# A projected column's residual: ScalarE reads the column twice, GpSimd subtracts, VectorE keeps the first stream's columns

## The reference

```
q = heads(q_in @ wq + bq)
k = heads(k_in @ wk + bk)
scores = einsum('bhqd,bhkd->bhqk', q, k) / sqrt(16)
```

## Time and profile before

| | us |
|---|---|
| median of three runs | 1411.68 (1407.81 to 1411.82) |
| span of the profiled execution, first to last instruction | 1379.5 |
| PE busy / VectorE / ScalarE / GpSimd, of the span | 1255.7 / 888.8 / 663.2 / 523.9 |

### The profile page before, as it was taken

The page is one execution under the profiler, slowest core; times in us unless marked ns, Lnnn a source line. Parts: engine busy times, 40 slices in busy tenths (PEclk is TensorE's granted clock), DMA queues, the critical chain, the costliest instruction groups (busy, mean ns, idle before and its releaser), DMA issues. The chain is left out here.

```text
span 1379.5 us, 18247 instructions
## 1 busy us (share of the span) xinstructions
PE 1255.7 (91%) x5694; PEld 569.1 (41%) x5694; DVE 888.8 (64%) x2045; ACT 663.2 (48%) x1243; POOL 523.9 (38%) x731
## 2 busy tenths in 40 slices
PE   6898989989999999999999999998899888999996
PEld 3232433323343224453453444443242334666663
DVE  5889789788877986458557567568768423233332
ACT  2355455566555655556546556446656551012221
POOL 4444251163312411326217227225423122456665
PEclk9799999999999999999999999999999999999998
DMA  8472513324330333033123123124622004934341
GB/s 262 131 245 81 159 49 96 109 65 147 110 106 24 108 93 108 22 87 108 47 63 108 47 62 108 47 62 123 139 85 48 17 16 118 337 99 55 55 54 16
DMA packets 113216, 131.53 MB, mean 95 GB/s; under 512 B 17017, under 2 KB 93305, under 8 KB 112867
## 3 DMA queue, kind: packets, MB, share of 16 engines
q1 hardware_dynamic: 102867, 119.91, 30.0%
q0 software_dynamic: 10256, 10.45, 4.6%
HBM read 83.25 MB, written 48.40 MB: 95 GB/s over the span
## 5 line engine op out<-in xcount | busy, mean ns | idle before, releaser
L1288 DVE TENSOR_REDUCE Mx<-bank 128x1 f32<-128x512 f32 x512 | 339.0, 685 | 206.6 <-PE bank L1022 204.5
L904 ACT ACTIVATE prob<-bank 128x512 f32<-128x512 f32 x576 | 332.4, 594 | 257.2 <-PE bank L1048 255.6
L1048 PE MATMUL bank<-QS,KS 99*128 99x512 bf16 x768 | 296.1, 387 | 40.1 <-ACT prob L904 19.5
L1022 PE MATMUL bank<-KS,QS 96*128 96x512 bf16 x768 | 296.9, 388 | 14.2 <-DVE Mx L1285 8.0
L1061 PE MATMUL bank<-prob,V 128*17 128x512 f32 x1536 | 206.6, 610 | 0.7 <-ACT prob L904 0.7
L904 ACT ACTIVATE prob<-prob 128x512 f32<-128x512 f32 x192 | 120.9, 629 | 159.4 <-DVE prob L1299 158.5
L1048 PEld LDWEIGHTS bank<-QS,KS 99*128 99x128 bf16 x768 | 74.8, 98 | 234.2 <-ACT prob L904 130.3
L1022 PEld LDWEIGHTS bank<-KS,QS 96*128 96x128 bf16 x768 | 76.0, 99 | 123.0 <-issue 47.2
L1285 DVE CUSTOM_DVE_ANT_0 bank<-bank,ff_h 128x512 f32<-128x512 f32 x128 | 87.9, 696 | 20.6 <-PE bank L1022 20.0
L741 POOL TENSOR_SCALAR parts<-rest 128x512 bf16<-128x512 f32 x47 | 29.1, 620 | 183.4 <-DVE rest L1248 182.8
L727 POOL TENSOR_SCALAR shift<-mv 128x4 f32<-128x4 f32 x28 | 5.5, 197 | 233.5 <-DVE mv L1209 233.5
(11 more groups left out here) (180 smaller groups left out, 1833.2 us busy)
## 6 DMA issues: line engine op xcount, KB each, us to landing
stack_scr<-parts SPq DMA_DIRECT2D x48, 384.0 KB, 2.6
QS<-stack_scr SPq DMA_DIRECT2D x47, 384.0 KB, 4.1
KS<-stack_scr SPq DMA_DIRECT2D x47, 384.0 KB, 5.0
stack_scr<-parts SPq DMA_DIRECT2D x48, 256.0 KB, 2.9
w_gu<-in_gate_up SPq DMA_DIRECT2D x16, 512.0 KB, 9.6
stack_scr<-parts SPq DMA_DIRECT2D x48, 128.0 KB, 2.9
cT<-in_ctxT SPq DMA_DIRECT2D x8, 512.0 KB, 5.8
w_dn<-in_down SPq DMA_DIRECT2D x16, 256.0 KB, 10.0
```

Of the source, the lines that this page charges most:

```text
L904: act.activation(prob[:, u % NP_, j, :], src, ACT.Exp, scale=CAST).then_inc(exp_done, 1)
L1022: pe.matmul(m, QS[0:STACK, h, qt * P:(qt + 1) * P], KS[0:STACK, h, :], start=True, stop=True).then_inc(s_full, 1)
L1048: pe.matmul(bankT[e % NT][:, :], KS[0:ROWS, h, kt * P:(kt + 1) * P], QS[0:ROWS, h, :], start=not on_pe, stop=True).then_inc(t_full, 1)
L1288: dve.tensor_reduce(dst, b, AX.X, ALU.max).then_inc(s_read, 1)
```

## The change

For all streams but the first (44 of the 48 columns):

- ScalarE reads the column twice, in two instructions one behind the other: once for part 0 (bf16), once as a whole with the bias into `rest` (fp32). The second frees the M bank, and counts in ScalarE's `m_read`; `head_ready` isn't counted any more.
- GpSimd waits for that count instead of VectorE's, subtracts part 0 from `rest` in place (a third instruction ahead of its two), and goes on as before.
- VectorE does nothing for these columns. In `jobs_read` the bank now goes back at `head`, not at `cut`.

Stream 0's four columns stay as they were.

```diff
--- before.py
+++ after.py
@@ -322,7 +322,10 @@
     read_by_act = {"hT": "turn", "aT": "attT", "relu": "ff1", "swish": "gate"}
     if kind in read_by_act:
         return "act", [(read_by_act[kind], *at)]
-    made = {"val": "v", "cut": "col", "i8turned": "i8T", "top": "logits", "route": "rank"}
+    if kind in ("head", "cut"):
+        return ("dve", [("col", *at)] if kind == "cut" else []) if at[0] == 0 else \
+            ("act", [("col", *at)] if kind == "head" else [])
+    made = {"val": "v", "i8turned": "i8T", "top": "logits", "route": "rank"}
     if kind == "add":
         return "dve", [("out", *at)]
     if kind == "i8add":
@@ -738,6 +741,8 @@
                         return
                     s, r = parts[:, j % 2, :, :], rest[:, j % 2, :]
                     read_done(pool, ("col", n, what, m))
+                    if n:
+                        link(pool.tensor_tensor(r, r, s[:, 0, :], ALU.subtract))
                     link(pool.tensor_scalar(s[:, 1, :], r, 1.0, 0.0, ALU.mult, ALU.add))
                     pool.tensor_tensor(s[:, 2, :], r, s[:, 1, :], ALU.subtract).then_inc(part_ready, 1)
 
@@ -868,8 +873,12 @@
                     if j >= 2:
                         act.wait_ge(part_out[j % 2], 48 * (j // 2))
                     act.wait_ge(m_full, i + 1)
-                    act.activation(parts[:, j % 2, 0, :], bankM[BANK[("col", n, what, m)]][:, :], ACT.Identity,
-                                   bias=b_qk[:, n // B, "qk".index(what), m:m + 1]).then_inc(head_ready, 1)
+                    b, bias = bankM[BANK[("col", n, what, m)]][:, :], b_qk[:, n // B, "qk".index(what), m:m + 1]
+                    if n:
+                        act.activation(parts[:, j % 2, 0, :], b, ACT.Identity, bias=bias)
+                        act.activation(rest[:, j % 2, :], b, ACT.Identity, bias=bias).then_inc(m_read["act"], 1)
+                    else:
+                        act.activation(parts[:, j % 2, 0, :], b, ACT.Identity, bias=bias).then_inc(head_ready, 1)
 
                 def minus(i):
 
@@ -1362,7 +1371,7 @@
                         largest(*at)
                     elif kind == "merge":
                         merge(*at)
-                    elif kind == "cut":
+                    elif kind == "cut" and at[0] == 0:
                         cut(*at)
                     elif kind == "val":
                         take_values(*at)
```

## The result

| | before | after |
|---|---|---|
| median of all runs on one chip, us | 1411.59 (1407.81 to 1413.62, 6 runs) | 1420.92 (1416.99 to 1423.35, 6 runs) |
| ratio | 1 | 1.0071, 95% interval 1.0052 to 1.009 |

The change makes the kernel 0.7% slower, 9.3 us. I had forecast no difference, 1411, with a range that ended at 1420.

The account below looks back on a forecast made before the run. The prediction took TensorE, nearly full and working in order, to bound the kernel through its stalls. Its terms summed to +0.1 us on a 1379.5 us span; with 32.2 us outside it, 1411 us, no difference, range 1401 to 1420.

Parts of the forecast that it names:

- What bounds the kernel, and the prices: TensorE's stalls move all that follows; a second read costs 0.68 us, a GpSimd subtraction 1.2 us.
- The M bank, -4.4: In four columns a feed-forward product waits 1.1 us for VectorE's residual; the whole wait goes, 4.4 us.
- VectorE's late relief, -1.4: In 560 to 1150 us, dropped residuals give 0.69 us at two columns, 619.9 and 632.1 us: 1.4 us.
- ScalarE on the path, +7.2: Second reads delay exponentials by 0.58 us; in 20 columns this reaches TensorE, 9.1 us, taken at 80%: 7.2 us.
- GpSimd +2.5: The subtraction delays GpSimd's queue, so layer norm gains and scale and the int8 chain come later: 2.5 us, from 0 to 6.
- rival (2): ScalarE's T-bank loop decides: pushes also delay maxima, `prob` and output copies; late exponential waits 25 us or more; 1420; chance 0.26.
- SyncE, "+0.5 us, at this one group": SyncE sends parts before maxima; parts 1.2 us later make the maxima 0.55 us late at one group (333.96, 335.58): +0.5 us.
- VectorE's early relief, -4.3: At the 24 early columns, dropped residuals shorten TensorE's stalls for VectorE, seven by 0.34 to 0.69 us: 4.3 us.
- Rival (1): In the masked stretch VectorE's backlog reaches beyond unbroken runs: 11 us come through in place of 4.3; 1403; chance 0.34.
- The sum: -4.3 - 1.4 - 4.4 + 7.2 + 2.5 + 0.5 = +0.1 us on a span of 1379.5.
- My own sign of being wrong: The stretch up to 560 us shorter by over 6 us, or the late one longer by over 6.
- The rule on reads that block each other: Two-SBUF-input VectorE instructions and GpSimd reads of SBUF block each other; the new subtraction costs VectorE up to 8 x 0.22 us.

Follow-up runs that it names:

- relief: The changed kernel without ScalarE's second read and GpSimd's subtraction, the residual left out: 1413.48 us, ratio 1.0003 to the kernel before.
- base_again: The kernel before, unchanged, run again with a new profile: 1411.05 us, ratio 1.0001.
- four: The kernel before with the change applied only to the four columns whose product waited for the M bank: 1402.79 us, ratio 0.9939.
- new1: The kernel before with the change applied to stream 1's four columns alone: 1412.69 us, ratio 1.0003.
- reread: The kernel before with a second ScalarE read of each column of streams 1 to 11 into a spare tile: 1425.05 us, ratio 1.0087.

## Why the prediction was wrong

The time missed the stated range by 0.9 us and the forecast by 10, and I gave "slower" 0.26. By its own steps:

- **What bounds the kernel, and the prices.** Right: TensorE's stalls set the time, the second read takes 0.680 us and the subtraction 1.157.
- **The M bank, -4.4.** The mechanism was right and it is the part worth having; that the sum fits is luck. Three places gave 1.33 us each, more than the wait of 1.1, and the first 0.46: there the wait didn't go whole, for it became one of 0.63 us for the second read.
- **VectorE's late relief, -1.4: too high.** At the two columns *relief* gains 0.50 and 0.49 us over base_again (630.9 and 635.7 there), and gives 0.51 and 0.57 back at 642.4 and 643.8, at waits for ScalarE's exponentials and GpSimd's gains. *relief* is 1.0 us shorter than *four* in groups 24 to 28, but 0.58 of that is the M bank. I never asked whom TensorE meets next when it comes earlier.
- **ScalarE on the path, +7.2, GpSimd +2.5.** Near enough together: 10.4 in the changed kernel against 9.7. Six late columns have the 0.58 and three the 0.54 us that I had listed. The engine that ends a wait isn't always the one I named, so the two can't be told apart well. The waits for exponentials late, 12.5 to 18.0, are as forecast, not the 25 of rival (2): its time came, its mechanism didn't.
- **What had no term: the clock. This step failed, and weighs most.** I priced each stall at its length and put the clock at nothing, without a reason. The changed kernel stands at 1.2 GHz for 12 us more in the mean of its runs, an estimated 3.4 to 4.3 us; in the two halves of its trace the intervals under a spell give +3.1 and +1.4. How much of this the change causes isn't shown: kernels with no or four changed columns range from 20.5 to 30.7 us between groups 4 and 47, those with twenty or more from 23.9 to 41.0.
- **SyncE, "+0.5 us, at this one group": this step failed.** Where I had expected it the maxima are late, but by more: waits of 1.22 and 0.34 us at groups 13 and 14, where *new1* has none; their intervals are 1.9 longer, against 0.5. And the wait at group 2, 1.6 us longer than in base_again, which GpSimd's third instruction makes, I had at nothing.
- **VectorE's early relief, -4.3: too high.** At its places it gave 2.7 to 3.2 us. Rival (1), VectorE's backlog reaching further (11 us), is refuted by the same runs.
- **The sum.** Against the forecast's +0.1, groups 4 to 47 of the trace have 4.5 more for the clock, 1.4 for the maxima, 1.2 for VectorE and 0.8 for all else: 7.9, where the stages give 7.5 (the references of the halves differ). The wait at group 2 is of the size of the 1.7 of the 9.3 that is left, but the start and the end of the traces vary by more than that, so this stays open. My own sign of being wrong, over 6 us in one half, was too wide: +4.6 and +3.0 passed under it.
- **The rule on reads that block each other.** In the changed kernel the eight VectorE additions with two SBUF inputs take 1.110 us each in place of 0.911. That is the rule that I had named (the Trainium skill, SBUF — State Buffer, Who interferes with whom), and the trace agrees: they stretch beside GpSimd's work, by 8 x 0.2 = 1.6 us of VectorE's queue, in the late stretch, where it has room. But it isn't the new subtraction that they meet, as I had it. The three longest, 1.60 to 1.61 us, stand beside two of GpSimd's gains (L808), and *reread*, which adds nothing to GpSimd, has 1.141: a shift of the queues against each other is enough.

## What to carry to other kernels

When work moves between engines column by column, price each place and change only those that pay: here four of 44 columns gave 3.4 us in their trace and 4 to 8 in the time, and the other 40 together cost 11. A stall that goes is worth the distance to the next wait whose end doesn't move with it: late in this kernel, 1.0 us of relief came back within 13 us. A delay on an engine that looks idle has to be followed to the DMAs behind it, at the start of the program too. Before a longer or shorter wait is put down to a change, look whether a spell at the low clock ahead of it, in one of the traces alone, made TensorE late: here it made a wait for GpSimd 0.39 us long that is 1.65 without it. Take a second trace of the kernel before when two spans differ by more than their times do.

## What the runs showed of the hardware

- The granted clock drops from 2.4 to 1.2 GHz in spells of 3.4 us or several of them in a row, 20.5 to 41.0 us in all between groups 4 and 47 of kernels whose TensorE is busy for 89% (*after*) to 91% (before) of the span. A spell costs from nothing, where a later wait hides it (190.0 in base_again), to 1.6 us, and spells move between traces of the same code.
- Among the timed runs of one kernel, 1 us more at 1.2 GHz goes with 0.28 to 0.36 us more of time.
- A VectorE addition of two 128x512 fp32 tiles in SBUF takes 0.68 to 1.61 us, the longest beside two GpSimd additions.
- The same kernel's expert part had a piece of 32.6 us in one trace and none in another; I didn't find what ScalarE and SyncE stand for there.
